# Projections and attention by halves of the tokens, the second gate beside the first half's scores, and gates with exclusive backward scans

## The reference, cut to what matters

```
decay = exp(-exp(w)) * (0.5 + 0.5 * tf)          # tf: one sigmoid per sequence
ek  = exp(min(f, 30));  ekv = ek * f
forward and reverse:  a = a * decay + ekv_t;  b = b * decay + ek_t     # nf, df, nb, db
euk = exp(min(u + f, 30))
num = nf + nb - ekv + euk * f
den = df + db - ek  + euk
out = sigmoid(x) * num / max(den, 1e-8) * (0.8 + 0.2 * tf)
```

```
q, k, v = (x @ W.T for each of Wq, Wk, Wv), 16 heads of 16
w = softmax(q k' / 4 + causal mask);  x = x + (w v) @ Wo.T
```

## Time and profile before

| what | value |
|---|---|
| median of 3 runs | 790.84 us (790.29 to 790.85) |
| the profiled execution | 792.08 us, span 790.3 us |
| mean granted clock of PE in it | 0.842 of full |
| DVE busy, whole span | 444.5 us (56%) |
| DVE busy, 79.8 to 262.2 us (the attention loop) | 169.9 of 182.4 us |
| PE busy, same stretch | 134.6 of 182.4 us |
| ACT busy, same stretch | 104.7 of 182.4 us |

### The profile page before, as it was taken

How to read it: one execution, slowest core, us unless ns; L and a number is a source line. 1 busy time by engine, 2 the same in 40 slices (tenths; PEclk the granted TensorE clock), 3 DMA queues, 4 the chain that set the end, 5 groups by cost and what they waited for, 6 DMA issues and landing times.

```text
span 790.3 us, 14021 instructions
## 1 busy us (share of the span) xinstructions
PE 588.3 (74%) x5774; PEld 441.2 (56%) x5774; DVE 444.5 (56%) x607; ACT 358.6 (45%) x754; POOL 144.0 (18%) x87
## 2 busy tenths in 40 slices
PE   0066677867778716467999999998649999999990
PEld 0033445655555502145465565566649999999980
DVE  5796999988999596663774344433541111111113
ACT  5643556565574547676366645563322222222210
POOL 0000000000000054310105754530021212222210
PEclk9997567685776968755899999998759999999996
DMA  9300000000000100000000000000159898889815
GB/s 359 111 0 1 1 1 1 1 1 1 1 1 2 41 0 0 1 0 1 0 2 2 3 2 2 2 2 2 36 212 375 313 339 315 336 312 328 318 75 166
DMA packets 18272, 72.44 MB, mean 92 GB/s; under 512 B 4320, under 2 KB 9568, under 8 KB 14496
## 3 DMA queue, kind: packets, MB, share of 16 engines
q1 hardware_dynamic: 16000, 65.50, 22.8%
q0 software_dynamic: 2208, 6.03, 2.0%
HBM read 66.42 MB, written 5.11 MB: 91 GB/s over the span
## 4 chain that ended last, share of the span: by engine, by line
PE 54%; DVE 32%; ACT 8%; issue 4%; DMA 2%; SPq 0%; POOL 0%; DVEq 0%; POOLq 0%; ACTq 0%
PE PS L1243 45%; DVE arena L822 4%; DVE arena L823 4%; DVE nmx L924 3%; PE PS L1466 1%; PE PS L1280 1%; PE PS L1539 1%; PE PS L1534 1%; DVE arena L834 1%; DVE arena L827 1%; DVE R L842 1%; DVE arena L833 1%; DVE arena L1233 1%; DVE arena L1001 1%; DVE peak L1005 1%
## 5 line engine op out<-in xcount | busy, mean ns | idle before, releaser
L1243 PE MATMUL PS<-arena 128*128 128x128 f32 (+6 forms) x1684 | 207.9, 299 | 27.6 <-DVE arena L1001 13.5
L1243 PEld LDWEIGHTS PS<-arena 128*128 128x128 f32 (+3 forms) x1684 | 170.7, 175 | 59.0 <-issue 25.7
L522 ACT ACTIVATE arena<-PS,nmx 128x128 f32<-128x128 f32 (+1 forms) x128 | 52.1, 420 | 83.2 <-DVE nmx L924 83.2
L1218 DVE TENSOR_TENSOR R<-arena,PS 128x128 f32<-128x128 f32 x23 | 6.6, 287 | 134.7 <-ACT arena L765 134.7
L1243 PE MATMUL PS<-arena,R 128*128 128x256 f32 x276 | 63.5, 380 | 0.6 <-ACT arena L771 0.6
L1295 PE MATMUL PS<-ident,arena 128*128 128x128 f32 x192 | 38.3, 355 | 23.4 <-ACT A L509 21.8
L1243 PEld LDWEIGHTS PS<-arena,R 128*128 128x128 f32 x276 | 50.6, 190 | 6.9 <-issue 0.9
L415 POOL DMA_INDIRECT ypair<-arena,oid x23 | 22.7, 988 | 136.0 <-ACT arena L771 136.0
L1295 PEld LDWEIGHTS PS<-ident,arena 128*128 128x128 f32 x192 | 30.2, 185 | 29.9 <-issue 15.2
L389 POOL TENSOR_TENSOR arena<-arena 128x1024 f32<-128x1024 f32 x16 | 37.8, 2367 | 45.7 <-DVE arena L1073 37.2
L367 POOL TENSOR_TENSOR arena<-arena 128x1024 f32<-128x1024 f32 x2 | 6.7, 3370 | 210.4 <-ACT arena L563 210.4
(11 more groups left out here) (264 smaller groups left out, 1152.5 us busy)
## 6 DMA issues: line engine op xcount, KB each, us to landing
arena<-in_moe SPq DMA_DIRECT2D x23, 1408.0 KB, 6.6
arena<-in_moe SPq DMA_DIRECT2D x23, 768.0 KB
arena<-ypair SPq DMA_DIRECT2D x4, 512.0 KB, 5.3
inproj<-in_inproj SPq DMA_DIRECT2D x1, 1344.0 KB, 10.5
arena<-in_fT SPq DMA_DIRECT2D x1, 1024.0 KB, 5.0
xT<-in_xT SPq DMA_DIRECT2D x1, 1024.0 KB, 5.4
R<-in_w1T SPq DMA_DIRECT2D x1, 1024.0 KB, 7.4
R<-in_w2T SPq DMA_DIRECT2D x1, 1024.0 KB, 9.4
```

What stands on the lines that cost most here:

```text
L522: sc.activation(pr[u % 2][:, j, 0:n], PS[:, 2 * (u % 2) + j // 2, (j % 2) * 256:(j % 2) * 256 + n], ACT.Exp, bias=nmx[:, u % 2, j:j + 1], ...
L1243: last = mm(dst, l, r, start=(n == 0), stop=(n == len(pairs) - 1))
```

## The change

- Halves in turn: PE makes q, k and v of half 0, runs units 0 to 15 (half 0), then makes q, k and v of half 1 and runs units 16 to 31. Before the projections of half 1 the pipeline of units is run empty (w = 16, 17 and `project(3)`); the scores of unit 16 wait for their copies. `keys_values` is cut into `keys` and `values`, with four slices of gates between the last adds of half 0 and the copies of half 1.
- Gate 1 goes from in front of the attention into the loop: only its step 1 stays ahead, and the slices are now gates 1 to 7, 35 in all, numbered n = u in half 0, n = 16 to 19 between the halves, n = u + 4 in half 1. A slice n with k = n % 5 does step 0, step 2, step 3, steps 5 and 6, or step 1 of the next gate. `gate(0, 1)` follows slice 3. `inputs(1)` (fc and ekv of half 1) moves behind `ternary_scales`.
- The reverse scans are exclusive: a cell of zero is set at the last token and the scan runs over the other 1023 with add first and multiply second, so that the term at the token itself is not counted twice. The subtraction of ek and ekv falls away with that. Step 4 is gone (one addition is left, in step 0), and the maximum with 1e-8 is folded into step 5. ACT makes it for itself for its guess by a Relu with bias -1e-8 and a logarithm with bias 1e-8.
- All gates use one set of sums buffers. POOL's clearing of the padding of `vv` no longer waits for gate 1. The buffers `pt` of half 0 lie in the places of half 1's q and k, since `A` is still needed.
- ACT makes its guess of gate 0 ahead of the three Abs passes over the weights (L472) and no longer does `bonus(1)` and `decay(2)` there.

```diff
-        sums = [[arena[:, w:w + K] for w in range(8 * K, 13 * K, K)],
-                [arena[:, w:w + K] for w in (18 * K, 19 * K, 20 * K, 21 * K, 27 * K)]]
-        dmats = [sb(f"dmat{i}", [P, N + 1]) for i in range(2)]
+        sums = [arena[:, w:w + K] for w in range(8 * K, 13 * K, K)]
+        tiny = sb("tiny", [P, 2])
+        dmats = [sb(f"dmat{i}", [P, N]) for i in range(2)]
         wter = arena[:, 27 * K:30 * K].bitcast(BF).rearrange("p (w n) -> p w n", w=3)
...
-        kT = halves(15)
-        qT = [halves(13).rearrange("p a (c n) -> p c a n", c=NCH), R[:, 0].rearrange("p c (a n) -> p c a n", a=CT)]
+        def by_half(o):
+            return arena[:, o * K:(o + 2) * K].rearrange("p (c a n) -> p c a n", c=NCH, a=CT)
+
+        qT, kT = [by_half(13), R[:, 0].rearrange("p c (a n) -> p c a n", a=CT)], by_half(15)
...
-        pt = [A[:, i, :] for i in range(2)]
+        pt = [[arena[:, 14 * K:15 * K], arena[:, 16 * K:17 * K]], [A[:, i, :] for i in range(2)]]
...
-            pool.wait_ge(S["dve_R"], 2)
             pool.memset(vv[:, :, :, HD:VW], 0.0).then_inc(S["pool_pad"], 1)
...
             def bonus(i):
                 m, c = divmod(i, 2)
-                if i >= 2:
-                    act.wait_ge(S["dve_num"], 1 if i == 2 else i)
+                if i:
+                    act.wait_ge(S["dve_num"], i)
                 for ct in range(CT):
                     cols = slice(ct * HALF, (ct + 1) * HALF)
-                    sc.activation(sums[i == 1][0][:, cols], fT[:, c, cols], ACT.Exp, bias=wu[:, m, 1, ct:ct + 1])\
+                    sc.activation(sums[0][:, cols], fT[:, c, cols], ACT.Exp, bias=wu[:, m, 1, ct:ct + 1])\
                         .then_inc(S["act_euk"], 1)
...
             def reciprocal_guess(i):
 
-                db, df = sums[i == 1][4], sums[i == 1][3]
+                db, df = sums[4], sums[3]
                 act.wait_ge(S["dve_den"], i + 1)
-                done(sc.activation(db, df, ACT.Ln))
+                done(sc.activation(db, df, ACT.Relu, bias=tiny[:, 0:1]))
+                done(sc.activation(db, db, ACT.Ln, bias=tiny[:, 1:2]))
                 sc.activation(db, db, ACT.Exp, scale=-1.0).then_inc(S["act_guess"], 1)
 
             bonus(0)
-            bonus(1)
-            decay(2)
+            reciprocal_guess(0)
...
-            reciprocal_guess(0)
...
-            reciprocal_guess(1)
+            bonus(1)
...
+            def queries(c):
+                for mt in range(CT):
+                    act.wait_ge(S["pe_q"], CT * c + mt + 1)
+                    for e in range(2):
+                        sc.activation(qT[e][:, c, mt, :], bank(mt), ACT.Copy, scale=hmask[:, e:e + 1]).then_inc(S["act_q"], 1)
...
+            def weigh(u):
...
-                if u >= 1:
-                    pt_copy(u - 1)
-                if u % 2 and u >= 3:
-                    turned_sums(u // 2 - 1)
-                i, k = divmod(u, FRAME)
-                if k == 1 and i < 6:
-                    bonus(i + 2)
-                if k == 3:
-                    reciprocal_guess(i + 2)
-                if k == 4 and i + 3 < 8:
-                    decay(i + 3)
-            pt_copy(31)
-            turned_sums(15)
+
+            def gate_part(n):
+                i, k = 1 + n // FRAME, n % FRAME
+                if k == 1:
+                    reciprocal_guess(i)
+                if k == 2 and i < 7:
+                    decay(i + 1)
+                if k == 3 and i < 7:
+                    bonus(i + 1)
+
+            for c in range(2):
+                queries(c)
+                for w in range(16):
+                    u = 16 * c + w
+                    weigh(u)
+                    if w:
+                        pt_copy(u - 1)
+                    if w % 2 and w >= 3:
+                        turned_sums(u // 2 - 1)
+                    if u + 4 * c < 7 * FRAME:
+                        gate_part(u + 4 * c)
+                pt_copy(16 * c + 15)
+                turned_sums(8 * c + 7)
+                if c == 0:
+                    for n in range(16, 20):
+                        gate_part(n)
...
-            for w in dmats:
-                done(v.memset(w[:, N:N + 1], 0.0))
+            done(v.memset(tiny[:, 0:1], -1e-8))
+            done(v.memset(tiny[:, 1:2], 1e-8))
...
-                g, nf, nb, df, db = sums[i == 1]
+                g, nf, nb, df, db = sums
                 src = ek if k == 1 else ekv
                 dmat = dmats[i % 2]
                 if k in (1, 2):
                     dve.wait_ge(S["act_decay"], 4 * (i + 1))
                     fwd, bwd = (df, db) if k == 1 else (nf, nb)
                     done(v.tensor_tensor_scan(fwd, dmat[:, 0:N], src[:, c, :], 0.0, ALU.mult, ALU.add))
-                    done(v.tensor_tensor_scan(bwd[:, ::-1], dmat[:, 1:N + 1][:, ::-1], src[:, c, ::-1], 0.0,
-                                              ALU.mult, ALU.add), "dve_scan")
+                    done(v.memset(bwd[:, N - 1:N], 0.0))
+                    done(v.tensor_tensor_scan(bwd[:, 0:N - 1][:, ::-1], src[:, c, 1:N][:, ::-1], dmat[:, 1:N][:, ::-1], 0.0,
+                                              ALU.add, ALU.mult), "dve_scan")
                 if k == 0:
                     dve.wait_ge(S["act_euk"], CT * (i + 1))
-                    done(v.scalar_tensor_tensor(g, g, E30, ek[:, c, :], ALU.min, ALU.subtract), "dve_g")
+                    done(v.scalar_tensor_tensor(df, g, E30, df, ALU.min, ALU.add))
+                    done(v.tensor_tensor(df, df, db, ALU.add), "dve_den")
                 if k == 3:
-                    done(v.tensor_tensor(nf, nf, nb, ALU.add), "dve_nf")
-                    done(v.tensor_tensor(g, g, fc[:, c, :], ALU.mult))
+                    done(v.scalar_tensor_tensor(g, g, E30, fc[:, c, :], ALU.min, ALU.mult))
+                    done(v.tensor_tensor(nf, nf, nb, ALU.add))
                     done(v.tensor_tensor(nf, nf, g, ALU.add), "dve_num")
-                if k == 4:
-                    done(v.tensor_tensor(df, df, db, ALU.add))
-                    done(v.tensor_tensor(df, df, g, ALU.add))
-                    done(v.tensor_scalar(df, df, 1e-8, None, ALU.max), "dve_den")
                 if k == 5:
 
                     dve.wait_ge(S["act_guess"], i + 1)
-                    done(v.tensor_tensor(df, df, db, ALU.mult))
+                    done(v.scalar_tensor_tensor(df, df, 1e-8, db, ALU.max, ALU.mult))
                     done(v.scalar_tensor_tensor(df, df, 2.0, db, ALU.subtract, ALU.mult))
                 if k == 6:
...
+            def keys(c):
                 for mt in range(CT):
                     dve.wait_ge(S["pe_k"], CT * c + mt + 1)
-                    done(v.tensor_copy(kT[:, mt, c * HALF:(c + 1) * HALF], bank(2 + mt)), "dve_k")
+                    done(v.tensor_copy(kT[:, c, mt, :], bank(2 + mt)), "dve_k")
...
+            def values(c):
...
             inputs(0)
             gate_step(0, 1)
             gate_step(0, 0)
-            gate_step(0, 4)
             gate_step(0, 2)
             gate_step(0, 3)
-            inputs(1)
             gate_step(0, 5)
             gate_step(0, 6)
             gate(0, 0)
+            ternary_scales()
+            inputs(1)
             gate_step(1, 1)
-            gate_step(1, 0)
-            gate_step(1, 4)
-            ternary_scales()
-            gate_step(1, 2)
-            gate_step(1, 3)
-            gate_step(1, 5)
-            gate_step(1, 6)
-            gate(0, 1)
-            keys_values(0)
...
-            keys_values(1)
+            keys(0)
+            values(0)
...
-            for u in range(32):
...
-                if u % 2 and u >= 3:
-                    inverse_sums(u // 2 - 1)
...
-                if u % 2 == 0 and u >= 4:
-                    normalise(u // 2 - 2)
-                if u in (1, 2, 3):
-                    ternary(u - 1)
-                if u % 4 == 0 and u >= 8:
-                    add_attention(u // 4 - 2)
-
-                i, k = divmod(u, FRAME)
-                if k < 2 and i:
-                    gate_step(i + 1, (5, 6)[k])
-                if i < 6:
-                    for part in ((), (1,), (0, 4), (2,), (3,))[k]:
-                        gate_step(i + 2, part)
-            inverse_sums(15)
-            normalise(14)
-            add_attention(6)
-            normalise(15)
+
+            def gate_part(n):
+                i, k = 1 + n // FRAME, n % FRAME
+                for part in ((0,), (2,), (3,), (5, 6), ())[k]:
+                    gate_step(i, part)
+                if n == 3:
+                    gate(0, 1)
+                if k == 4 and i < 7:
+                    gate_step(i + 1, 1)
+
+            for c in range(2):
+                for w in range(16):
+                    u = 16 * c + w
+                    if w % 2 and w >= 3:
+                        inverse_sums(u // 2 - 1)
+                    maxima(u)
+                    if w % 2 == 0 and w >= 4:
+                        normalise(u // 2 - 2)
```

(66 more changed lines are left out.)

25 lines of the change are left out of this document (10 added, 15 removed).

## The result

The changed kernel takes 770.68 us (median of four, 769.84 to 772.71), the kernel before 790.85: ratio 0.9759, 95% interval 0.9742 to 0.9776, so 20.2 us faster. Forecast were 776.4 us in a range of 768.5 to 785, 14.4 us faster. The profiled execution has a span of 769.5 us, where the sum had given 775.9.

The account below looks back on a forecast made before the run. The DVE's work was taken to bound the attention loop. First maximum 48.0 + list 185.1 + boundary 8 + waits inside 6.7 = 247.8 us at the last maximum's end, before 262.2; 14.4 saved, median 790.84 to 776.4, range 768.5 to 785.

Parts of the forecast that it names:

- Prices of the gates: DVE time per gate: 19.6 us instead of 21.4, net 1.76 us less; reverse scan taken at 2.29 us.
- the rival on the other side: Reverse scan with add first is slower, at the upper bound of 4.6 us making the kernel 813 us; chance 0.04.
- Start: Ahead of the loop: `gate(0, 0)` ends at 33.5 us, first maximum at 48.0 instead of 79.8.
- The DVE's list: DVE instructions from the first to the end of the last maximum, gaps included: 185.1 us.
- Boundary: DVE waits between the two halves: 5.8 to 9.5 us, taken as 8, mostly before the second key copy.
- Waits inside: DVE waits for PE inside the halves, mainly at projecting units 7, 11, 23, 27 and short slices: 6.7 us.
- Drain: The stretch right behind the last maximum: unchanged at 10.7 us.
- the main case: The forecast's own case: 771 to 783 us, with waits from 9 to 21 us; chance 0.65.
- The split by cause: Of 14.4 us saved, 14.1 come from the gates; the start's shorter wait (about 8) is given back at the boundary.
- PE as the bound: Rival: PE becomes the bound, waits inside the halves 14 us and at the boundary 10: 786 us; chance 0.11.
- The reverse scan and the table: Two rivals: slower reverse scan, up to 813 us, chance 0.04; Relu switching ACT's table, 781 us, chance 0.04.
- An evenly fed PE with more clock: Rival: PE's clock rises, waits inside the halves 1 us, boundary 5.8: 768.5 us; chance 0.13.

Follow-up runs that it names:

- again2: The changed kernel run once more, unaltered, as partner on the same chip for other versions: 770.38 us, ratio 0.9748.
- max_on_dve: The changed kernel with the maximum with 1e-8 back on the DVE as its own operation, without ACT's Relu pass: 777.14 us, ratio 0.9847.
- no_sum: The changed kernel without the DVE pass adding the two scans of ekv in gates 1 to 7, not replaced: 767.79 us, ratio 0.9717.

## Why the prediction was right, point by point

- **Prices of the gates**: right. The reverse scan with add first costs 2.29 us, so the rival on the other side falls; a memset 0.06 instead of 0.09; Relu caused no table load; its pass took 1.15 us, not 1.06, which hid.
- **Start**: first maximum forecast at 48.0, seen at 47.8; gate 0 ready at 33.5 in both; no wait for the guess or the sigmoid.
- **The DVE's list**: forecast 185.1, seen 185.1.
- **Boundary**: forecast 5.8 to 9.5 and taken as 8, seen 6.8. In `again2` it was 8.5, so the term is right within its spread. PE made q and k at full clock in 7.0 us, the low end. The parts were less right than their sum: the wait for the guess was 2.55 us (forecast 1.3 to 2.4), that for the second key only 1.61 (3 to 6, which left out that the DVE copies the first key meanwhile; 2.74 in `again2`), and that for the scores of unit 16 2.11 instead of 1.2. So the boundary's idle time was not "mostly in front of the second key copy".
- **Waits inside**: forecast 6.7, seen 4.0. This is the largest mis-sized term. It was 4.0 in all three profiles of this kernel. Of the four projecting units only 7 and 23 made the DVE wait (1.02, 1.01), in `again2` 11 and 23 (1.15, 0.88), so it is not the length of the slice alone that decides; the short slices cost nothing. In the last two units it was 1.97 where I had 0.4.
- **Drain**: forecast 10.7, seen 9.9 at full clock. **Behind**: forecast unchanged at 517.4, seen 515.9, and 512.5 to 517.9 in three profiles of this same kernel.
- The span's difference is the sum of these: 0.2 + 1.2 + 2.7 + 0.8 + 1.5 = 6.4 us, and the median's 5.7. All terms erred to the same side, none made up for another. With 770.7 us and 10.8 us of waits the result lies at the edge of the main case (771 to 783, waits from 9 to 21), and the miss is two fifths of the gain that was forecast.
- **The split by cause was wrong**, though the sum was right: "14.1 are the 8 x 1.76 of the gates, and the shorter wait at the start (about 8) is given back at the boundary". On top of the halves the arithmetic does give 14.9 us, but alone it gives 7.9; and the halves are worth 4.1 us alone and 11.0 on top of the arithmetic, where the split has nothing. These 4.1 us are most of what the forecast missed. In the profiles the last maximum ends 5.3, 6.0 and, with both, 18.5 us earlier. The 7.2 us between (4.7 with `again2` for both): without the halves the two gates in front bring none of their 3.5 us, because ACT's guess then waits behind the Abs passes and PE's projections set the start; and in the loop the shorter list costs 5.2 us of new waits in the old order against 1.5 in the new one (12.7 less 7.5, 10.8 less 9.3; 3.2 with `again2`). The drain adds to it, 9.9 us with both parts and 12.1 and 13.0 with one, and the stretch behind takes as much back (515.9 against 512.7 and 516.3, before 517.4). That the new order waits less fits its having four projecting units inside a half, not six, with two of them under the longest slices; no run changed that alone, so it stays argued, and it speaks against it that unit 11, under a slice of two scans, made the DVE wait in `again2`.
- **Rivals.** PE as the bound: not in this kernel, where `max_on_dve` shows that added DVE time still counts in full, but with less of it PE and the drain take part back, as `no_sum` shows. The reverse scan and the table: both out, by the rows above. An evenly fed PE with more clock: in the loop the clock rose only from 0.69 to 0.70, the waits and the boundary came half of the way to that rival.

## What to carry to other kernels

Count the list of the bounding engine instruction by instruction: here the counted list of the changed loop matched the measured one within 0.1 us, and 3.9 of the 6.4 us of error sat in the waits, nearly all the rest behind the last maximum. Price a saving in the order in which it will run: the gates' shorter list was worth 7.9 us in one order of the work and 14.9 in another, so two edits on one engine should be timed alone and together. Where a pipeline is run empty between two halves, put first in the idle engine's list what the other engine waits for (here the adds), and last the copies that it needs only when it is through; here that was worth some 4 us. Take the spread of one kernel's profiles before reading the difference of two kernels: the waits of a loop moved by 1.7 us with nothing changed.

## What the runs showed of the hardware that was not expected

The feed-forward stretch, untouched by all these edits, comes in two lengths: 80.8 to 81.9 us at a granted PE clock of 0.77 to 0.79 in eight of the profiles, and 84.1 to 84.5 us at 0.70 to 0.76 in the other six. The changed kernel shows both, here in the table by stretch, first in its own profile and then in that of `again2`:

```profile
284.64:368.77 84.13, 52.78 (x247) 31.60 (x249) 52.14 (x74) 52.18 (x73) 22.48 (x9) 0.76 0.00 1
```

```profile
286.29:367.17 80.88, 51.11 (x252) 29.86 (x253) 52.12 (x73) 53.26 (x74) 22.46 (x9) 0.79 0.00 1
```

These 3.3 us lie behind everything that was changed and are about half of what the stretch behind the attention varies by (511.6 to 518.2 us over all profiles). What decides between them was not found. The drain's length goes with the clock as well, in the new order from 9.9 us at full clock over 11.2 at 0.91 to 12.9 to 13.4 at 0.87 and 14.6 at 0.77. Part of that is more work, since the window holds 122 matmul records at full clock and 128 at 0.87 and 0.77.
